# Graph convolutions on one core: node blocks finished in a loop of their own behind the edge loop, in place

## What is computed

```python
def conv(h, W, b):
    m = jnp.concatenate([h[dst], h[src], edge_attr], axis=1) @ W + b
    return jax.ops.segment_sum(m, dst, num_segments=n_nodes)
h = jax.nn.relu(conv(x, W1, b1))
h = jax.nn.relu(conv(h, W2, b2))
return conv(h, W3, b3)
```

## Time and profile before

| | |
|---|---|
| median of 3 runs | 8498.54 us (8495.15 to 8500.81) |
| the profiled execution's own time | 8507.21 us |
| its span in the trace | 8505.5 us |
| pass 0, from the first sum of `p_z` to the last in its loop | 150.4 to 1799.1 us |
| pass 0, what is behind its loop | 1799.1 to 1844.5 us |
| pass 1 | 1844.5 to 2936.5 us |
| pass 2 | 2936.5 to 4020 us |
| norms and PNA layers | 4020 to 8505.5 us |

### The profile page before, as it was taken

The page is one execution under the profiler, slowest core; times in us unless marked ns, Lnnn a source line. Parts: engine busy times, 40 slices in busy tenths (PEclk is TensorE's granted clock), DMA queues, the critical chain, the costliest instruction groups (busy, mean ns, idle before and its releaser), DMA issues. The chain is left out here.

```text
span 8505.5 us, 168699 instructions
## 1 busy us (share of the span) xinstructions
PE 6896.0 (81%) x53894; PEld 5588.3 (66%) x53895; DVE 4530.8 (53%) x6206; ACT 2272.7 (27%) x3543; POOL 5718.6 (67%) x5876
## 2 busy tenths in 40 slices
PE   4888888878989788897688878888868888888885
PEld 3666666667888678887566656666646666666663
DVE  6776766752222222222566656655655665666665
ACT  3555555530000000000222222222232222222223
POOL 3555555547777577775677777777737777777773
PEclk9999999988888798997799989898979898998897
DMA  4454544567777777776222222222222222222222
GB/s 154 178 187 172 187 183 172 188 218 281 271 271 286 238 285 265 283 284 219 89 69 72 68 69 76 66 69 70 73 64 71 68 69 70 73 69 66 70 73 62
DMA packets 417849, 1231.99 MB, mean 145 GB/s; under 512 B 122068, under 2 KB 221774, under 8 KB 369024
## 3 DMA queue, kind: packets, MB, share of 16 engines
q1 hardware_dynamic: 217273, 748.98, 24.7%
q0 software_dynamic: 187232, 233.06, 11.4%
q10 hardware_dynamic: 13160, 248.08, 7.4%
HBM read 948.13 MB, written 281.51 MB: 145 GB/s over the span
## 5 line engine op out<-in xcount | busy, mean ns | idle before, releaser
L1857 POOL DMA_INDIRECT data<-q_rows,idx x3328 | 3156.4, 948 | 1148.1 <-issue 999.6
L905 POOL DMA_INDIRECT data<-h_parts,idx x2508 | 2524.3, 1006 | 1446.4 <-issue 948.7
L1029 PE MATMUL p_z<-hs,adj 128*128 128x192 bf16 x22442 | 2149.0, 254 | 57.1 <-issue 57.1
L1029 PEld LDWEIGHTS p_z<-hs,adj 128*128 128x128 bf16 x22442 | 1961.7, 101 | 328.0 <-issue 129.1
L1989 ACT COPY back<-p_back 128x1024 f32<-128x1024 f32 x418 | 423.3, 1013 | 2365.6 <-PE p_back L1877 2365.6
L2059 DVE TENSOR_TENSOR_SCAN run<-reset,run,p_turn 128x1024 f32<-128x1024 bf16 x416 | 974.4, 2342 | 147.4 <-PE p_turn L1924 140.8
L1128 ACT CAST adj<-p_count 128x1012 bf16<-128x1012 f32 x836 | 898.4, 1103 | 307.7 <-PE p_count L1016 300.6
L573 DVE TENSOR_TENSOR hot<-p_ramp,ends 128x2048 f32<-128x2048 f32 x416 | 950.0, 2284 | 0.2
L1883 PE MATMUL part<-hot,t 128*128 128x128 f32 x6688 | 908.4, 294 | 45.4 <-issue 45.4
L1883 PEld LDWEIGHTS part<-hot,t 128*128 128x128 f32 x6688 | 877.6, 212 | 46.0 <-issue 46.0
L1888 PE MATMUL part<-hot,back 128*128 128x128 f32 x6688 | 815.2, 275 | 0.0
(11 more groups left out here) (308 smaller groups left out, 6392.4 us busy)
## 6 DMA issues: line engine op xcount, KB each, us to landing
adj<-counted SPq DMA_DIRECT2D x304, 1568.0 KB
counted<-adj ACTq DMA_DIRECT2D x76, 3136.0 KB
reset<-flags SPq DMA_DIRECT2D x208, 512.0 KB
data<-q_rows,idx POOLq DMA_INDIRECT x3328
data<-h_parts,idx POOLq DMA_INDIRECT x2508
feat<-in_ea_blocks SPq DMA_DIRECT2D x208, 128.0 KB
ea<-in_ea_cols SPq DMA_DIRECT2D x154, 88.0 KB, 1.9
rden<-node_rows SPq DMA_DIRECT2D x50, 256.0 KB
```

The source lines that it names most:

```text
L905: pool.indirect_dma_start(out=data[:, p % HELD, j, 0:PARTS], out_offset=None, in_=table[:, :], in_offset=bass.IndirectOffsetOnAxis(ap=idx[ ...
L1029: mm = pe.matmul(p_z[:, 0:PARTS], adj[:, (q + LAG) % 2, hi, :], hs[:, hi, :], start=(hi == 0), stop=(hi == BLOCKS - 1))
L1857: pool.indirect_dma_start(out=data[:, r, j, :], out_offset=None, in_=q_rows[:, :], in_offset=bass.IndirectOffsetOnAxis(ap=idx[:, r, j:j + ...
```

## The change

In pass 0 no quad is finished inside the edge loop. The loops over quads stand once behind the edge loop, over all 25, on TensorE, ScalarE, VectorE and SyncE. VectorE writes the results into `hs` in place of the old features, and SyncE stores from there. Pass 1 finds its features in `hs` and does not load them. In addition the `turn` of the last P group of a turn moves on TensorE into the next turn's first `dense` (as the other P groups' already stood), with its `finish` on VectorE behind the next turn's first pair; semaphore counts shift by one for it (`BEFORE`), and one further `turn` and `finish` (`pos` -1) are issued: the first adds zeros. Passes 1 and 2 keep their order, and pass 2 still loads `hs`.

```diff
@@ conv_pass
+    nth[-1] = -1
+    BEFORE = 1 if first else 0
@@ SyncE
             def store(n):
                 sp.wait_ge(s_h, n + 1)
-                sp.wait_ge(s_out, n * 16 + 32)
+                if not first:
+                    sp.wait_ge(s_out, n * 16 + 32)
                 gate(sp)
-                sp.dma_start(by_partition(out_rows)[:, bass.ds(n * QUAD, QUAD), :],
-                             out[:, bass.ds((n & 1) * QUAD, QUAD), :]).then_inc(s_out, 16)
+                of = hs[:, bass.ds(n * QUAD, QUAD), :] if first else out[:, bass.ds((n & 1) * QUAD, QUAD), :]
+                sp.dma_start(by_partition(out_rows)[:, bass.ds(n * QUAD, QUAD), :], of).then_inc(s_out, 16)
...
-            else:
+            elif layer > 1:
                 for n, loaded in enumerate(s_hs):
...
-            finished_quads(sp, quads_of(sp, chip.quads, KT - 1), store)
+            if first:
+                with sp.Fori(0, QUADS) as n:
+                    store(n)
+            else:
+                finished_quads(sp, quads_of(sp, chip.quads, KT - 1), store)
@@ TensorE, turn
-                pe.wait_ge(s_added, k * H + (n + 1))
+                pe.wait_ge(s_added, k * H + (n + 1 + BEFORE))
@@ TensorE, the loop
-                        if pos == POS_P[-1]:
+                        if pos == POS_P[-1] and not first:
                             turn(k, pos)
                             finished_quads(pe, finished, convolve, banks_read)
...
-                        if pos - 1 in POS_P:
+                        if pos - 1 in POS_P or first:
                             between[0 if first else 1] = lambda pos=pos: turn(k, pos - 1)
...
             if first:
+                turn(KT, -1)
                 dense(KT, 0, count=False)
-                scatter(KT, 0, KT * H + 1)
+                scatter(KT, 0, KT * H + (1 + BEFORE))
...
-            finished_quads(pe, quads_of(pe, chip.quads, KT - 1), convolve)
+            if first:
+                with pe.Fori(0, QUADS) as n:
+                    convolve(n)
+            else:
+                finished_quads(pe, quads_of(pe, chip.quads, KT - 1), convolve)
@@ VectorE, rows
-                to = out[:, bass.ds((n & 1) * QUAD, QUAD), :]
-                part = lambda m: out[:, bass.ds((n & 1) * QUAD, QUAD), m * D:(m + 1) * D]
+                part = lambda m: (hs[:, bass.ds(n * QUAD, QUAD), m * D:(m + 1) * D] if first else
+                                  out[:, bass.ds((n & 1) * QUAD, QUAD), m * D:(m + 1) * D])
...
-                v.wait_ge(s_out, n * 16 + 16)
+                if first:
+                    v.wait_ge(s_turned, n + 1)
+                else:
+                    v.wait_ge(s_out, n * 16 + 16)
@@ VectorE, the loop
-                                if i == 2 and pos - 1 in POS_P:
+                                if i == 2:
                                     finish(k, pos - 1)
...
+                finish(KT, -1)
                 sum_z(KT, 0)
...
-            nodes(quads_of(v, chip.quads, KT - 1))
+            nodes(None if first else quads_of(v, chip.quads, KT - 1))
```

More of the change, by code:

```diff
@@ L717, in conv_pass @@
         far_high = conv[:, :, :].rearrange("p b f -> p (b f)").bitcast(F16)[:, 0:BLOCKS * WX]
-        out = sb("out", [P, 2 * QUAD, D], F32) if last else sb("out", [P, 2 * QUAD, PARTS], BF16)
+        out = sb("out", [P, 2 * QUAD, D], F32) if last else None if first else sb("out", [P, 2 * QUAD, PARTS], BF16)
         wa = sb("wa", [D, D])
@@ L865, in turn @@
                         bring_next(k, POS_E.index(pos))
-                finished_quads(sp, quads_of(sp, chip.quads, k - 1), store)
+                if not first:
+                    finished_quads(sp, quads_of(sp, chip.quads, k - 1), store)
             if not first:
@@ L959, in far @@
                               start=(i == 0), stop=(i == GC - 1)).then_inc(s_far_count, 1)
-                if not first:
+                if layer > 1:
                     for loaded in s_hs:
@@ L1026, in dense @@
                             gate(pe)
-                        if not first and hi % HS_PIECE == 0:
+                        if layer > 1 and hi % HS_PIECE == 0:
                             pe.wait_ge(s_hs[hi // HS_PIECE], 16)
@@ L1040, in scatter @@
                 pe.wait_ge(s_dense_added, k * NQ + (q + 1))
-                pe.wait_ge(s_nodes, k + 1)
+                if not first:
+                    pe.wait_ge(s_nodes, k + 1)
                 pe.wait_ge(s_added, added)
@@ L1172, in summed @@
                 def summed():
-                    act.wait_ge(s_added, k * H + 1)
+                    act.wait_ge(s_added, k * H + (1 + BEFORE))
                     act.wait_ge(s_dense_added, k * NQ + (LAG + 1))
-                finished_quads(act, quads_of(act, chip.quads, k - 1), stage, summed)
+                if first:
+                    summed()
+                    with act.Fori(0, QUADS) as n:
+                        stage(n)
+                else:
+                    finished_quads(act, quads_of(act, chip.quads, k - 1), stage, summed)
             further_windows_of(act, further)
@@ L1259, in sum_places @@
                 v.wait_ge(s_part, k * H + (H + n + 1))
-                v.wait_ge(s_by_feature, k * H + (n + 1))
+                v.wait_ge(s_by_feature, k * H + (n + 1 + BEFORE))
                 if first:
@@ L1273, in finish @@
                 base = begin_of(k, pos) if base is None else base
-                rows, at = (slice(0, M), M) if pos in POS_P else (slice(D, KC), EA)
+                rows, at = (slice(D, KC), EA) if pos in POS_E else (slice(0, M), M)
                 to = acc[rows, window(base, 0)]
-                v.wait_ge(s_by_feature, k * H + (n + 2))
-                v.wait_ge(s_added, k * H + (n + 1))
+                v.wait_ge(s_by_feature, k * H + (n + 2 + BEFORE))
+                v.wait_ge(s_added, k * H + (n + 1 + BEFORE))
                 v.wait_ge(s_dense_added, k * NQ + (dense_before(pos + 1) + 1))
@@ L1375, in rows @@
                  .then_inc(s_step, 1)
-                v.wait_ge(s_out, n * 16 + 16)
+                if first:
+                    v.wait_ge(s_turned, n + 1)
+                else:
+                    v.wait_ge(s_out, n * 16 + 16)
                 if last:
+                    to = out[:, bass.ds((n & 1) * QUAD, QUAD), :]
                     v.wait_ge(s_step, n + 1)
@@ L1400, in nodes @@
             def nodes(finished):
-                finished_quads(v, finished, rows)
+                if first:
+                    with v.Fori(0, QUADS) as n:
+                        rows(n)
+                else:
+                    finished_quads(v, finished, rows)
                 v.memset(scratch[:, 1:2], 0.0).then_inc(s_nodes, 1)
@@ L1449, in _ @@
                         for q in done_with(pos):
-                            finish_dense(k, q, k * H + (nth[pos] + 1), dense_begin[q])
-                        if pos == POS_P[-1]:
+                            finish_dense(k, q, k * H + (nth[pos] + 1 + BEFORE), dense_begin[q])
+                        if pos == POS_P[-1] and not first:
                             finish(k, pos, begin)
```

17 lines of the change are left out of this document (9 added, 8 removed).

## The result

The changed kernel takes 8434.2 us (median of 4 runs, 8432.5 to 8450.2), the kernel before 8498.7 us beside it (4 runs, 8495.2 to 8500.8): ratio 0.9925 [0.9913, 0.9938], 64.5 us less. The forecast of 8368 us has twice that gain; it is 66 us too fast, and the result lies outside its range, 8326 to 8398. The profiled execution took 8450.2 us.

The account below looks back on a forecast made before the run. Pass 0 was taken as bound by TensorE, pass 1 as set by GpSimd's gathers. A loop gain of 239.0 us less a tail loss of 108.3 us gave 130.7 us, hence 8368 us, range 8326 to 8398.

Parts of the forecast that it names:

- Crossing, 19.6 us: Pass 0's step into the next turn, without quads: 19.6 us each, 18 of them 353 us, bounds 18.4 and 21.2.
- 2.73 us: Crossing in pass 0: VectorE's late return from its branch back, expected to stay at 2.73 us.
- 1.59 us: Crossing in pass 0: VectorE's wait for TensorE's last count, taken as slack hiding 1.59 us of the branch.
- rival 2: Crossings in pass 0 keep a stall and the low clock, 25.75 us each: 111 us more, 8479 us, chance 0.07.
- Queues: Pass 0: gathers and `counted` writes come closer together but carry no cost, as in inside steps at DMA share 0.59.
- Inside steps, 55.6 us a turn: Pass 0's three steps within a turn: 18.42, 18.75 and 18.43 us, the third losing 1.4 us.
- Tail, 153.7 us: From pass 0's 76th sum to pass 1, with 25 quads at 5.21 us: 153.7 us for 45.4, a 108.3 us loss.
- Pass 1, 0: Start of pass 1: not making five 960 KB loads gains 0, since GpSimd's gathers set the pass.
- forecast of the loop: Pass 0's edge loop: 1409.7 us against 1648.7, a gain of 239.0 us.
- Rival 1: Quads behind the loop: TensorE gets 2.4 GHz, 3.6 us a quad, 38 us less, 8330 us, chance 0.12.
- Rival 3: Loop over 25 quads: VectorE stalls at each branch, 5.8 to 6.0 us a quad, 17 us more, 8385, chance 0.12.
- Rivals 4 and 5: Pass 1 does gain, 8351 to 8364 us, chance 0.04; quads behind the loop do not overlap, 8579 us, chance 0.03.

Follow-up runs that it names:

- late_write: Changed kernel with each turn's fourth `counted` write in pass 0 issued in the next turn, behind ScalarE's third copy; 8347.4 us, ratio 0.9818.
- unrolled: Changed kernel with VectorE's 19 turns of pass 0 written out, so no branch back there; other engines keep their loops; 8322.4 us, ratio 0.9786.
- hs_load2: Changed kernel with pass 1 fetching the `hs` features by its own loads, as before; 8437.3 us, ratio 0.9921.
- unrolled_warm4b: Changed kernel with VectorE's pass 0 turns written out and four unused 506-column products added to each quad, faster chip; 8293.9 us, ratio 0.9751.
- unrolled_warm2b: Changed kernel with VectorE's pass 0 turns written out and two unused 506-column products added to each quad, faster chip; 8347.5 us, ratio 0.9816.
- turn_back: Changed kernel with the last P group's turn and finish back at the end of its turn, quads still behind the loop; 8497.5 us, ratio 0.9995.
- moved_alone2: Kernel before with only the last P group's turn moved into the next turn, quads still inside the loop, faster chip; 8457.3 us, ratio 0.9943.
- moved_alone: Kernel before with only the last P group's turn moved into the next turn, quads still inside the loop, slower chip; 13125.8 us, ratio 0.9967.

## Why the prediction was wrong

- **Crossing, 19.6 us: the step that failed.** It was put together as "18.5 + 2.73 - 1.59", and the 2.73 us were taken from the earlier trace rows. Measured 23.9 us on average ((1474.4 - 19 x 55.0) / 18), so 18 x 4.3 = 77 us. The 2.73 us are the idle time of a branch back when no `counted` write is in flight; the change puts the branch 0.8 us behind the write's issue, and then the branch takes 7.06 us instead of 2.8 to 3.1, VectorE's idle time in it 5.47 us (late_write: 1.35 with the write moved away; unrolled: no stall at all with the branch taken away). The lower clock behind it adds some 0.7 us. Nor are the 1.59 us slack: VectorE waits exactly as long at that place in inside steps and in this crossing too (at 465.00). What is really hidden is smaller: in late_write 1.35 us of idle time make the step 0.65 us longer (18.95 for 18.30 us). Without the write's packets in the way the forecast's 19.6 us would have been 0.8 us too long.
- **The row that told it was there.** The earlier trace rows show 6.43 us idle behind the first branch back, in the only crossing without a quad, which is what every crossing becomes. It was set against the 2.73 us of the earlier trace rows as if the latter were the rule and it the exception, and put into rival 2 with a chance of 0.07. The DMA view of that stall (212.5 to 218.8) has the write in it:

```profile
q10 hardware_dynamic: 64, 1.20, 52.2%
```

  What rival 2 named, "a stall and the low clock", happened, at 23.9 us and not 25.75: the wait for the turn did go, as said there. Rival 2 did not say why the stall was longer there.
- **Queues.** "The gathers and the writes of `counted` ... carry no cost" was right of the data (unrolled: 18.1 us a step) and left out a third user of the DMA engines, the instructions.
- **Inside steps, 55.6 us a turn**: right, 55.0; the third step lost its 1.4 us.
- **Tail, 153.7 us**: right, 152.0; 5.21 us a quad and granted clock 0.50 held over 25 quads. The prediction took this from four quads that it called gapless (the earlier trace rows have TensorE busy for 21.51 of 22.26 us); over the 25 there is no gap at all.
- **Pass 1, 0**: right (hs_load2, 1091.0 and 1093.3 us).
- **The sum**: forecast of the loop missed by +64.7 us, tail by -1.7, pass 1 by +1.3; the medians were off by 8434.2 - 8367.8 = 66.4. The profiled execution was off by 73.7; its further 9 us lie behind the start of pass 2, and it was the slowest of the four.
- **Rival 1** (the quads at full clock) didn't happen. That it is the work and not the gaps is shown by unrolled_warm4b against unrolled_warm2b, which differ in two products a quad and are both gapless. By the rule of the Trainium skill weighed in the prediction (TensorE: Matmul & The Clock Gate, "Why this matters for your kernels"), keeping the engine busy without a break would have been enough; 130 us of gapless quads at 0.50 say that it isn't for such products.
- **Rival 3** didn't happen: in the loop over 25 quads all 24 distances are 5.21 us, and from that short loop's branch (L1428) to the next record are 0.2 us. **Rivals 4 and 5**: no sign of either.
- **The parts singly**: quads behind the loop alone bring nothing (turn_back), the moved turn alone 47 us (moved_alone2), both 64 to 70. So as measured, the gain is mostly the turn's. But the quads' leaving brings little only because it puts the branch behind the write: with the write out of the way (late_write) the two together bring 156 us, 110 more than the turn alone, and that is more than the 131 us forecast.

How long the fetch is held up can be read from the packet records. The write is eight packets of 25 KB, one after another and about 1 us each, on each of the 16 DMA engines. In the change (branch at 443.72) the fetch starts at 448.99 on an engine that has moved five of its eight; the write's last data packet ends at 452.6. In turn_back the branch comes when about three of the eight are done, and the fetch starts at 461.92, behind all of them, the last packet but for one of 4 bytes. That is why the branch is as slow 4.1 us behind the write's issue as 0.8 us behind it: it lets about five packets pass in both. Left open is why three of the eight stay behind the fetch in the change; no run here shows it.

## What to carry to other kernels

A loop's branch back can cost a fetch (here on VectorE in the edge loop of pass 0), and the fetch goes through the DMA engines: before pricing it, look at which large transfer is in flight at that place before the change and which will be after it, and take the duration from a crossing that looks like those to come, even if there is only one. When most crossings are of one kind and one is of another, the odd one is not noise. And when a long run of small products sits at half the clock, try what it would be with a few wide ones among them: here four a quad, which do nothing, made the kernel 28 us faster, and two a quad made it 25 us slower (8347.5 for 8322.4 us).

## What the runs showed of the hardware

- VectorE's branch back in the edge loop of pass 0, from the branch to its next record: 2.8 to 3.1 us where no bulk write is in flight (before, late_write, moved_alone2), 6.3 to 7.1 us where a 3.1 MB write to memory was issued 0.8 to 5.2 us earlier (the change, turn_back, and the one crossing without a quad of before and of moved_alone2). VectorE's idle time in it is 1.15 to 3.05 us and 4.65 to 6.9 us.
- The fetch is one 8 KB packet on a queue of its own (q14). It starts 1.0 to 1.3 us behind the branch where no write runs, and 5.3 us behind it in the change (4.1 us in its first crossing).
- The branch of the same loop in passes 1 and 2 takes 0.3 us to the next record, in every kernel. VectorE has 114 to 150 instructions in such a turn, against 321 in pass 0 of the change; that this is the reason is not shown.
- Granted clock 0.50 over some 130 us in which TensorE had no gap, with 28 small products a quad; 1.00 with four of 506 columns added, 0.50 with two added. The quads' pace is the same on both chips (5.21, 3.81 and 6.17 us).
- One chip ran the kernel before in 13178 us (24 runs), another in 8504 us. On the slower one the inside steps of pass 0 are 28.2 to 28.6 us long on average (moved_alone), on the faster one 18.3 to 19.0 us (moved_alone2); the mean granted clock is 0.75 against 0.88. Why is not known.
